# Home numbers for every expert in the dispatched rows, and one column of them fetched for each expert tile

## The chip, the cores and the metric

The kernel runs on one core of one Trainium2 chip. The metric is the device time of one execution in microseconds (us), the median of three runs. A core has TensorE (PE in the profile; PEld are its weight loads), VectorE (DVE), ScalarE (ACT), GpSimd (POOL) and SyncE (SP), and 16 DMA engines that serve the queues of all of them. SP only issues DMAs here, POOL issues the indirect ones.

## What is computed

Two transformer-like layers on one sequence of 2048 tokens of width 256, in float32. What matters here is the second:

```python
xn = _layernorm(x)
x = x + _L1_attn_ref(xn, W, b) + _L1_ffn_ref(xn, w_router, we1, we3, we2, ws1, ws3, ws2)

# _L1_ffn_ref: 16 experts, each token goes to its best 4
probs = softmax(xt @ w_router)
top_w, top_i = top_k(probs, 4)
top_w = top_w / sum(top_w)
g = silu(xt @ we1[e]) * (xt @ we3[e])          # 256 -> 128 for each expert e
moe_out = sum over the token's experts of top_w * (g @ we2[e])
shared = silu(xt @ ws1) * (xt @ ws3) @ ws2
out = shared / 5 + moe_out * 4 / 5
```

The attention of layer 1 is linear (one vector of sums over all tokens). Layer 0 has softmax attention with 16 heads and its own mixture of 16 experts with the best 2.

## The kernel before

Three stages follow each other, each a block of programs, one for each engine; the end of a block holds all engines until the last has finished.

**stage_first** (to about 602 us) is layer 0. Its work is interleaved by a planner written in Python. Only one step of it is touched: at a certain point SP clears rows of the scratch tensor xd1 in HBM (`clear`, L366 and L922).

**stage_second** (603 to 731 us) projects the attention output of layer 0, normalizes the 16 token tiles of 128 rows (four chunks of TC = 4 tiles), and routes. For each chunk VectorE picks the best four experts (`best_of`, which signals masks_ready), TensorE counts ranks (`ranks`, ranks_ready), and VectorE turns them into slots (`slots_of`, slots_ready): for each token and choice k the row of xd1 to which it goes. xd1 holds a region of CAP = 2048 + 128 rows for each expert. POOL then dispatches: for each chunk, choice and token tile one indirect DMA scatters 128 rows of `xn` (256 values, a one, and one more number) to xd1, 64 scatters in all. The additional number is the *home*: the row of yd1 where the result of this token and choice is to be written, token * 4 + k plus an offset. As it depends on k, POOL rewrites this column of xn for two tiles before each pair of scatters, and must first wait until the pair's earlier scatters have landed (L1848). SP meanwhile loads weights, copies padding rows behind the end of each expert's region (L1826), waits for the tables of the expert tiles (tables_ready) and for the whole dispatch (L1833), and loads the first four expert tiles into the ring `xs` (L1835). TensorE's main work from 651 on is the shared feed-forward part, 16 units (`shared`); VectorE multiplies each (`gated`).

**stage_experts** (731 us to the end) runs over NT1 = 79 tiles of 128 dispatched rows, each of one expert. For tile j TensorE transposes the rows of `xs` (L1694), ScalarE copies them out, TensorE makes the hidden part (L1702, eight products) with the weights that VectorE and ScalarE copied to `w_now` (L1569), ScalarE and VectorE make silu and product, TensorE the output (L1711), VectorE copies it to `ys` (L1651), and POOL scatters it to yd1 by the home numbers (L1682). The home numbers of a tile are made by POOL (L1676): the home column of xs, or a row of the ring's own dump area where the row is padding (it reads zero there). SP loads tile j into the ring of YRING = 4 as soon as tile j - 4 is transposed and its home numbers are made (L1582, L1583). The loop is unrolled by BODY = 16; at its head SP loads the first rows of the next 16 tiles into registers (L1576). After the loop the results are fetched in token order, weighted, summed and stored (L1588 to L1666), while TensorE makes the rest of the shared part.

## Time and profile before

| | |
|---|---|
| median of three runs | 906.23 us (905.91 to 911.66) |
| profiled execution | 906.89 us, its span 905.2 us |
| busy in the span: PE, DVE, ACT, POOL | 830.5, 645.3, 468.8, 437.1 us |
| stage_first, stage_second, stage_experts begin (first work on TensorE of the last two) | 0, 603.0, 731.3 us |
| mean granted TensorE clock | 0.96 of full speed |
| DMA packets, bytes | 70182, 110.05 MB |

Times in the rows are microseconds from the start of the span. The time between profiled time and span (1.7 us) lies outside the first and last instruction. The granted clock is 1.00 at 2.4 GHz and 0.50 at 1.2 GHz. A bracket at the end of a timeline row says how long the engine was idle before it and what ended the idle time; "issue" means that the profile shows nothing for which it waited.

### The profile page before, as it was taken

How to read it: one execution, taken by the hardware profiler on the slowest of the kernel's cores; microseconds unless marked ns; L12 is line 12 of the kernel's file. 1: busy time of each engine (PE TensorE's matmuls, PEld its weight loads, DVE VectorE, ACT ScalarE, POOL GpSimd, SP SyncE). 2: the span in 40 equal slices, each digit the busy share in tenths (PEclk: the TensorE clock that was granted, in tenths of full speed). 3: DMA queues.
4: the chain of work that ended last, by engine and by line, in shares of the span. 5: the costliest groups of instructions: out<-in, count | busy, mean ns of one | idle time of the engine just before them, and what ended most of it. 6: DMA issues, size and time to landing. Idle time of an engine off the chain costs nothing. (4 is left out here: it accounts for less than half of the span.)

```text
span 905.2 us, 16683 instructions
## 1 busy us (share of the span) xinstructions
PE 830.5 (92%) x4934; PEld 449.4 (50%) x4935; DVE 645.3 (71%) x1472; ACT 468.8 (52%) x883; POOL 437.1 (48%) x720
## 2 busy tenths in 40 slices
PE   5978699999988999999999998989999989999993
PEld 3533133334533444444444432138644769888982
DVE  5587988898867888888788888437547336555648
ACT  2643154556654666666565666754313046555547
POOL 3422045603652433653435446531578848878820
PEclk9997698999998999999999999989999989999997
DMA  9654772210272121272211222325852235555566
GB/s 328 212 129 137 207 142 89 89 46 25 81 128 71 49 61 56 80 127 71 70 38 38 55 60 76 93 65 188 302 166 88 88 117 164 157 154 159 158 255 246
DMA packets 70182, 110.05 MB, mean 122 GB/s; under 512 B 16662, under 2 KB 49942, under 8 KB 69590
## 3 DMA queue, kind: packets, MB, share of 16 engines
q1 hardware_dynamic: 49430, 54.04, 22.9%
q0 software_dynamic: 16000, 45.70, 14.7%
q10 hardware_dynamic: 4672, 9.34, 3.4%
q8 instruction: 38, 0.62, 0.3%
q14 instruction: 42, 0.34, 0.1%
HBM read 62.53 MB, written 46.22 MB: 120 GB/s over the span
## 5 line engine op out<-in xcount | busy, mean ns | idle before, releaser
L1275 DVE TENSOR_REDUCE part_max<-ps_row 128x1 f32<-128x512 f32 (+3 forms) x560 | 353.6, 670 | 71.1 <-PE ps_row L1429 38.7
L1139 ACT ACTIVATE probs<-ps_st 128x1024 f32<-128x1024 f32 (+3 forms) x320 | 278.2, 896 | 204.6 <-PE ps_st L1408 188.2
L1333 PE MATMUL ps_o<-probs,v_all 128*17 128x512 f32 (+3 forms) x1280 | 150.4, 542 | 6.9 <-POOL probs L1009 5.6
L1429 PE MATMUL ps_row<-ks,qs 96*128 96x512 bf16 (+3 forms) x320 | 110.2, 379 | 13.7 <-DVE part_max L1275 9.3
L1429 PE MATMUL ps_row<-xt_ks,qs 96*128 96x512 bf16 (+3 forms) x320 | 104.5, 354 | 6.9 <-DVE part_max L1275 6.5
L1682 POOL DMA_INDIRECT yd<-moe_ys,moe_home x79 | 82.6, 1046 | 25.5 <-POOL moe_home L1676 13.4
L1408 PE MATMUL ps_st<-qs,ks 99*128 99x512 bf16 (+3 forms) x320 | 88.7, 360 | 2.9 <-DMA qs<-max_parts 2.7
L1408 PE MATMUL ps_st<-qs,xt_ks 99*128 99x512 bf16 (+3 forms) x320 | 85.7, 356 | 3.9 <-ACT probs L1139 2.8
L1702 PE MATMUL moe_ps_h<-moe_xs_t,moe_w_now 128*128 128x128 f32 x632 | 86.0, 280 | 1.3 <-ACT moe_xs_t L1607 0.8
L1702 PEld LDWEIGHTS moe_ps_h<-moe_xs_t,moe_w_now 128*128 128x128 f32 x632 | 78.4, 195 | 3.2 <-DVE moe_w_now L1569 2.0
L1429 PEld LDWEIGHTS ps_row<-ks,qs 96*128 96x128 bf16 x320 | 31.9, 100 | 95.6 <-DVE part_max L1275 52.8
L1009 POOL TENSOR_SCALAR_AFFINE_SELECT probs<-probs 128x256 f32<-128x256 f32 x128 | 52.8, 419 | 47.3 <-ACT probs L1139 46.0
L1851 POOL DMA_INDIRECT xd<-xn,slot x64 | 65.8, 1029 | 19.0 <-issue 15.9
L1019 POOL TENSOR_SCALAR moe_h_tanh<-moe_h_tanh 128x128 f32<-128x128 f32 x47 | 25.0, 532 | 98.7 <-ACT moe_h_copy L1151 98.5
L1429 PEld LDWEIGHTS ps_row<-xt_ks,qs 96*128 96x128 bf16 x320 | 31.0, 97 | 80.7 <-DVE part_max L1275 46.6
L1642 DVE TENSOR_TENSOR moe_hid_t<-moe_ps_h,moe_act 128x128 f32<-128x128 f32 x79 | 23.0, 291 | 47.7 <-ACT moe_act L1614 37.2
L997 POOL DMA_INDIRECT xd<-o_t,slot x32 | 31.4, 982 | 46.2 <-ACT probs L1139 41.7
L1432 PE MATMUL ps_row<-mask,ident 128*128 128x128 bf16 x256 | 51.7, 227 | 0.0
L1711 PE MATMUL moe_ps_y<-we,moe_hid_t 128*128 x158 | 48.6, 389 | 3.1 <-DVE moe_hid_t L1642 1.6
L1408 PEld LDWEIGHTS ps_st<-qs,xt_ks 99*128 99x128 bf16 x320 | 27.3, 99 | 47.8 <-ACT probs L1139 27.0
L1029 POOL DMA_DIRECT2D yd<-moe_ys x47 | 28.5, 605 | 46.1 <-DVE moe_ys L1267 45.4
L1333 PEld LDWEIGHTS ps_o<-probs,v_all 128*17 128x17 f32 x1280 | 21.7, 95 | 53.6 <-issue 29.0
(288 smaller groups left out, 1307.3 us busy)
## 6 DMA issues: line engine op xcount, KB each, us to landing
moe_xs<-xd SPq DMA_DIRECT2D x79, 129.0 KB
qk_parts<-probs SPq DMA_DIRECT2D x16, 384.0 KB, 4.2
qs<-qk_parts SPq DMA_DIRECT2D x96, 64.0 KB, 2.5
moe_xs<-xd POOLq DMA_DIRECT2D x47, 128.0 KB, 2.4
yd<-moe_ys POOLq DMA_DIRECT2D x47, 128.0 KB, 2.1
xd<-zeros POOLq DMA_DIRECT2D x2, 2048.0 KB, 15.5
moe_w<-in_w ACTq DMA_DIRECT2D x2, 2048.0 KB
w<-in_we SPq DMA_DIRECT2D x8, 512.0 KB
```

Of the source, the lines that this page charges most:

```text
L997: pool.indirect_dma_start(out=m.xd0, out_offset=bass.IndirectOffsetOnAxis(m.r["slot"][:, choice, i:i + 1], 0), in_=m.xn[:, i, :], in_offse ...
L1009: pool.affine_select(out=corner, in_=corner, compare_op=ALU.is_ge, fill=keep, base=0, pattern=[[0, 2], [1, P]], channel_multiplier=-1).the ...
L1139: act.activation(probs[:, at % NPB, :, off:CH], ps_st[at % 2][:, :, off:CH], ACT.Exp, scale=HD ** -0.5).then_inc(exp_done, 1)
L1275: dve.tensor_reduce(part_max[reduced % 2][:, h:h + k, i, j:j + 1], bank[:, 0:k * w].rearrange("p (h w) -> p h w", h=k), AX_X, ALU.max).the ...
L1333: mm = pe.matmul(ps_o[32 * q:32 * q + HD + 1, off:CH], m.v_all[:, k, g * HG + q, :], probs[:, (at + q // 2) % NPB, q % 2, off:CH], start=F ...
L1408: mm = pe.matmul(ps_st[n % 2][:, h, off:CH], ks[g % 2][:, q, k * P:(k + 1) * P], qs[c][:, q, off:CH], start=True, stop=True)
L1429: mm = pe.matmul(cols, qs[c][0:KROWS, h, i * P:(i + 1) * P], ks[g % 2][0:KROWS, h, j * CH:j * CH + w], start=True, stop=(j < c))
L1432: mm = pe.matmul(cols[:, w - P:w], m.ident16[:, :], m.mask16[:, :], start=False, stop=True)
L1682: pool.indirect_dma_start(out=yd, out_offset=bass.IndirectOffsetOnAxis(home[:, k:k + 1].bitcast(U32), 0), in_=ys[:, k % U, :], in_offset=N ...
L1702: mm = pe.matmul(ps_h[b][:, part * P:(part + 1) * P], w_now[:, b, k, part * HID:(part + 1) * HID], xs_t[:, b, k, :], start=(k == 0), stop= ...
L1711: pe.matmul(ps_y[b][:, :], hid_t[:, b, :], w2[:, bass.ds(expert, 1), :], start=True, stop=True).then_inc(y_done, 1)
L1851: pool.indirect_dma_start(out=m.xd1, in_=xn[:, i, :], in_offset=None, out_offset=bass.IndirectOffsetOnAxis(r["slot"][:, k, i:i + 1], 0)).t ...
```

## The change

A row of xd1 now carries 16 home numbers, one for each expert (XW = D + 1 + E, 273 values instead of 258). For each chunk VectorE writes, for each token and expert e, token * 4 + (the choice k by which the token goes to e), from the masks of the choices, in three operations on 128 x 64 values (`homes_of`, at the start of `slots_of`). The numbers no longer depend on the choice that is being sent, so POOL writes no column and waits for no earlier dispatch: it issues the 64 scatters one after the other. In stage_experts SP loads the 256 values of each row and, by a second DMA of 128 pieces of 4 bytes, the one column that belongs to the tile's expert into `home` (`load_tile`). For this it loads the tile's expert into a register too. POOL's home numbers and the ring of dump rows go; the scatter of tile j takes the fetched column as its offsets and waits for the tile's loads (32 instead of 16). Padding rows and unused tiles get home numbers of their own in a larger dump area of yd1 (2 E tiles): SP writes them from `blank`, one DMA for the unused tiles, and the padding copies take the last block. The cleared part of xd1 grows from 1 block of 128 rows to 17.

```diff
-XW = D + 2
+XW = D + 1 + E
+PADS = E * (CAP + P)
...
-                        clear(sp, m, m.xd1, E * CAP // P, E * CAP // P + 1, m.cleared[1])
+                        clear(sp, m, m.xd1, E * CAP // P, PADS // P + 1, m.cleared[1])
...
+def load_tile(sp, m, b, j, first, expert):
+
+    sp.dma_start(m.xs[:, b, :], m.xd1[bass.ds(first, P), 0:D]).then_inc(m.x_in[b], 16)
+    sp.dma_start(m.home[:, j:j + 1] if isinstance(j, int) else m.home[:, bass.ds(j, 1)],
+                 m.xd1[bass.ds(first, P), bass.ds(expert + (D + 1), 1)].bitcast(I32),
+                 allow_slow_non_contiguous=True).then_inc(m.x_in[b], 16)
...
             def load_rows(j):
+                first_experts[:] = nc.values_load_multi_w_load_instructions(
+                    m.r["tile_e"][0:1, bass.ds(j + EPAD, BODY)], engines=[mybir.EngineType.SP], min_val=0,
+                    max_val=E - 1, skip_runtime_bounds_check_because=IN_RANGE)[1]
...
                 if there(j) and since(j, U):
                     sp.wait_ge(x_turned, j - (U - 1))
-                    sp.wait_ge(home_ready, j - (U - 1))
-                    sp.dma_start(xs[:, u % U, :], xd[bass.ds(first_rows[u], P), :]).then_inc(x_in[u % U], 16)
+                    load_tile(sp, m, u % U, j, first_rows[u], first_experts[u])
...
-            for j in range(tiles + 3):
-                if j < tiles:
-                    pool.wait_ge(x_in[j % U], 16 * (j // U + 1))
-                    pool.tensor_scalar(home[:, j:j + 1], xs[:, j % U, D + 1:XW], ring[:, j % U:j % U + 1], None,
-                                       ALU.max).then_inc(home_ready, 1)
-                k = j - 3
-                if k >= 0:
-                    pool.wait_ge(home_ready, k + 1)
-                    pool.wait_ge(y_copied, k + 1)
-                    pool.indirect_dma_start(out=yd, out_offset=bass.IndirectOffsetOnAxis(home[:, k:k + 1].bitcast(U32), 0),
-                                            in_=ys[:, k % U, :], in_offset=None).then_inc(y_out[k % U], 16)
+            for j in range(tiles):
+                pool.wait_ge(x_in[j % U], 32 * (j // U + 1))
+                pool.wait_ge(y_copied, j + 1)
+                pool.indirect_dma_start(out=yd, out_offset=bass.IndirectOffsetOnAxis(m.home[:, j:j + 1].bitcast(U32), 0),
+                                        in_=ys[:, j % U, :], in_offset=None).then_inc(y_out[j % U], 16)
...
-            sp.wait_ge(m.cleared[1], 16)
+            sp.wait_ge(m.cleared[1], 32)
+            sp.wait_ge(ones_ready, 3)
+            sp.dma_start(m.xd1[E * CAP:PADS + P, DP:XW].rearrange("(b p) h -> p b h", p=P), blank[:, :, :]).then_inc(m.cleared[1], 16)
+            sp.wait_ge(m.cleared[1], 48)
...
             for half in range(2):
                 sp.wait_ge(dispatched[half], 16 * TOP1 * T // 2)
+            experts = nc.values_load_multi_w_load_instructions(
+                m.r["tile_e"][0:1, EPAD:EPAD + YRING], engines=[mybir.EngineType.SP], min_val=0, max_val=E - 1,
+                skip_runtime_bounds_check_because=IN_RANGE)[1]
             for b, first in enumerate(rows):
-                sp.dma_start(m.xs[:, b, :], m.xd1[bass.ds(first, P), :]).then_inc(m.x_in[b], 16)
+                load_tile(sp, m, b, b, first, experts[b])
...
-                    for half in range(2):
-                        i = c * TC + 2 * half
-                        if k:
-                            pool.wait_ge(dispatched[half], 32 * (c * TOP1 + k))
-                        step.then(pool.tensor_copy(xn[:, i:i + 2, DP:XW], home[:, k, i:i + 2].unsqueeze(2)))
-                        for i in (i, i + 1):
-                            pool.indirect_dma_start(out=m.xd1, in_=xn[:, i, :], in_offset=None,
-                                                    out_offset=bass.IndirectOffsetOnAxis(r["slot"][:, k, i:i + 1], 0)
-                                                    ).then_inc(dispatched[half], 16)
+                    for i in range(c * TC, (c + 1) * TC):
+                        pool.indirect_dma_start(out=m.xd1, in_=xn[:, i, :], in_offset=None,
+                                                out_offset=bass.IndirectOffsetOnAxis(r["slot"][:, k, i:i + 1], 0)
+                                                ).then_inc(dispatched[i % 2], 16)
...
+            def homes_of(c):
+
+                k_hot, cs = r["hots"][c], slice(c * TC, (c + 1) * TC)
+                if c == 0:
+                    dve.wait_ge(homes_based, 1)
+                dve.wait_ge(masks_ready, c + 1)
+                step.then(dve.scalar_tensor_tensor(homes[:, :, :], k_hot[:, 2, :, :], 2.0, k_hot[:, 1, :, :], ALU.mult, ALU.add))
+                step.then(dve.scalar_tensor_tensor(homes[:, :, :], k_hot[:, 3, :, :], 3.0, homes[:, :, :], ALU.mult, ALU.add))
+                step.then(dve.tensor_tensor(xn[:, cs, DP:XW].bitcast(I32), homes[:, :, :],
+                                            home[:, cs].unsqueeze(2).to_broadcast([P, TC, E]), ALU.add))
+
             def slots_of(c):
 
+                homes_of(c)
                 chunk_slots(dve, step, r, c, ranks_ready, slots_ready)
```

## Rows read from the trace of the kernel before

**Rows 1.** Timeline of all engines at the hand-over to stage_experts: start, duration, engine, line.
```profile
725.96 0.97 POOL L1851 DMA_INDIRECT xd<-xn,slot  x1 [0.30 <-issue]
727.29 0.69 DVE L1992 TENSOR_TENSOR o_t<-ps_ab,gate 128x512 f32<-128x512 f32 x1 [2.74 <-issue]
728.66 1.95 SPq L1835 DMA_DIRECT2D moe_xs<-xd  x4
...
731.28 1.09 PE L1694 MATMUL moe_ps_x<-ident,moe_xs 128*128 128x128 f32 x4 [4.10 <-PEq L1734]
```

**Rows 2.** Windows of 1 us: busy time of each engine, granted clock, DMA share, GB/s.
```profile
core 0: us, PE busy (x) PEld busy (x) DVE busy (x) ACT busy (x) POOL busy (x), PEclk, DMA share, GB/s
...
604.00:605.00 1.00, 1.00 (x3) 0.75 (x3) 0.42 (x1) 0.00 (x0) 0.00 (x0) 0.50 0.28 62
...
729.00:730.00 1.00, 0.00 (x0) 0.00 (x0) 0.00 (x0) 0.00 (x0) 0.00 (x0) 0.98 0.26 61
...
736.00:737.00 1.00, 1.00 (x6) 0.97 (x5) 0.00 (x0) 0.25 (x1) 0.00 (x0) 0.61 0.54 140
```

**Rows 3.** POOL's two operations of an expert tile: duration ns min/median/max, first and last start.
```profile
L1682 POOL DMA_INDIRECT yd<-moe_ys,moe_home x79: 974/1047/1107, 738.5 to 866.2; - x79
L1676 POOL TENSOR_SCALAR moe_home<-moe_xs,moe_ring x79: 280/300/417, 731.6 to 861.3; 128x1 int32<-128x1 f32 x79
```

**Rows 4.** TensorE's timeline, the transposes of two expert tiles, four tiles apart.
```profile
750.99 0.38 PE L1694 MATMUL moe_ps_x<-ident,moe_xs 128*128 128x128 f32 x2
...
757.18 0.38 PE L1694 MATMUL moe_ps_x<-ident,moe_xs 128*128 128x128 f32 x2
```

**Rows 5.** Waits from 731 to 865: who for whom, us in total, times, longest.
```profile
PE moe_ps_h L1702 <- DVE moe_w_now L1569: 0.4, 1, 0.4
...
PEld moe_ps_h L1702 <- DVE moe_w_now L1569: 2.0, 4, 0.7
```

**Rows 6.** POOL's dispatch: the page's row (busy, mean ns, idle before), then its timeline.
```profile
L1851 POOL DMA_INDIRECT xd<-xn,slot x64 | 65.8, 1029 | 19.0 <-issue 15.9
...
625.89 1.01 POOL L1851 DMA_INDIRECT xd<-xn,slot  x1 [0.58 <-POOL xn L1849]
...
634.38 0.19 POOL L1849 CAST xn<-home 128x2 f32<-128x2 int32 x1 [3.46 <-DMA xd<-xn,slot]
```

**Rows 7.** Timeline of all engines at the hand-over from stage_first to stage_second.
```profile
601.88 0.59 ACT L1050 COPY masks<-ps_o 128x512 f32<-128x512 f32 x1 [1.18 <-PE ps_o L1333]
...
602.99 0.67 PE L2129 MATMUL ps_o<-count,o_t 128*128 128x256 f32 x2 [1.16 <-PEq L776]
```

**Rows 8.** POOL's timeline, the last scatter of the results.
```profile
866.18 0.97 POOL L1682 DMA_INDIRECT yd<-moe_ys,moe_home  x1 [0.30 <-issue]
```

**Rows 9.** VectorE's timeline in stage_second.
```profile
640.60 0.22 DVE L268 COPY given<-ps_l 128x64 f32<-128x64 f32 x1 [1.63 <-PE ps_l L246]
...
663.09 0.23 DVE L295 SCALAR_TENSOR_TENSOR weight<-weight,top_sum 128x64 f32<-128x64 f32 x1
```

**Rows 10.** TensorE's timeline, the transposes of tiles 12 and 13 in stage_second.
```profile
638.26 0.60 PE L2098 MATMUL ps_t<-ident,xn 128*128 128x128 f32 x4
```

**Rows 11.** SP in the loop over expert tiles: its waits, and its register loads.
```profile
SPq L1583 <- POOL moe_home L1676: 64.3, 65, 2.4
...
L1576 SPq TENSOR_LOAD <-tile_row x5: 284/977/990, 731.1 to 833.3; - x5
```

**Rows 12.** DMA issues: engine, count, KB each, median us from issue to landing.
```profile
moe_xs<-xd POOLq DMA_DIRECT2D x47, 128.0 KB, 2.4
...
xd<-zeros POOLq DMA_DIRECT2D x2, 2048.0 KB, 15.5
...
w_router<-in_w_router SPq DMA_DIRECT2D x1, 16.0 KB, 1.7
```

**Rows 13.** SP's timeline in stage_first around the clearing of xd1.
```profile
191.35 0.59 SPq L371 DMA_DIRECT2D xd<-zeros  x1
209.08 1.77 SPq L865 DMA_DIRECT2D qs<-max_parts  x3
```

**Rows 14.** VectorE's copies of the weights in the loop: ns min/median/max.
```profile
L1569 DVE COPY moe_w_now<-w x79: 293/351/569, 731.8 to 861.0; 128x256 f32 x79
```

41 lines of the change are left out of this document (20 added, 21 removed).

## The prediction

> **What bounds the kernel now.** I read the profile in the order in which the change touches it. First the page's 40 slices and the windows: TensorE is busy nearly without a break through both late stages, so a microsecond counts only if it moves TensorE or the hand-over from one stage to the next. Then the timeline of all engines at the hand-over from stage_second to stage_experts [rows 1]. VectorE's last product starts at 727.29 and ends at 727.98. POOL's last dispatch starts at 725.96, so its rows land after 727. SP waits for them, starts its first row load at 728.66 and is through with four of them at 730.61. Only then does every engine pass the end of the block: TensorE's first transpose is at 731.28, after 4.10 us of nothing. TensorE had ended at 727.18, VectorE at 727.98, so about 3 us of the pause belong to the dispatch and the loads behind it. The windows show a second price [rows 2]: the granted clock still reads 0.98 in 729 to 730, is 0.50 afterwards, and comes back within 736 to 737. The first expert tiles run at 1.2 GHz.
>
> In stage_experts the chain of waits names POOL from 807 on, scatter and home number in turn. That is a trap. POOL needs 1.05 us for a scatter and 0.30 for a home number [rows 3], and with the gaps about 1.56 per tile; TensorE passes four tiles in 757.18 - 750.99 = 6.19 us, 1.55 per tile [rows 4]. The two run side by side, but the waits of TensorE and its weight loads in this stretch name neither a transfer nor POOL; beside the hand-over the largest is 2.0 us in total for VectorE's weight copies [rows 5]. TensorE sets the pace and POOL only follows.
>
> **What the change removes.** (1) In the dispatch POOL now writes a home column (0.19 us) before each pair of scatters, and from the second choice on waits until the last scatters of these rows have landed; one such wait was 3.46 us [rows 6]. Without column and waits, 64 scatters take 1.03 us each in the mean and some 0.3 between them [rows 6], 85 us. From 625.89, and 0.75 later for the new VectorE work below, they end near 712. The last rows land before 716, and SP's eight short issues are done by about 720. That is 8 us ahead of VectorE's 727.98. The dispatch thus leaves the path, and the hand-over waits for VectorE. How long the block's end then takes is seen at the stage before: ScalarE ended at 602.47, TensorE began at 602.99, 0.52 us [rows 7]. So TensorE begins at 727.98 + 0.52 = 728.5 instead of 731.28: **-2.8 us**.
>
> (2) The pause shrinks from 4.1 to 1.3 us, and with it, I hold, the low clock disappears. The mean of 0.98 in 729 to 730 [rows 2] says that the clock was full until close to 730, 2.8 us into the pause. Against it: after the pause of 1.16 us at 602.99 [rows 7] the granted clock is 0.50 in 604 to 605 [rows 2]; but there TensorE came out of a stretch with gaps and narrow products, here out of one that the slices show as full. From 731.28 to the fourth tile's transpose near 737.1 pass 5.8 us. TensorE does in it two tiles' work less one output product, plus one pair of transposes: at the pace of 1.55 us [rows 4] about 2.9 us, and 0.6 that I allow for ScalarE's first copies, 3.5 in all. Bounds 0 and 2.5; I take **-2.3 us**, as the full clock at 729 to 730 is the nearer row.
>
> (3) In stage_experts 79 home numbers of 0.30 us [rows 3] leave POOL, and SP's wait for them. POOL drops to about 1.35 per tile, but TensorE's 1.55 stays: worth 0. The end also stays: the last scatter at 866.18 stood only behind its predecessor's issue, 0.30 us [rows 8], and no home number was there.
>
> **What it adds.** (4) VectorE makes the columns: three small operations on 128x64 per chunk. The nearest row is the scalar_tensor_tensor on 128x64, 0.23 us, 0.25 with its wait [rows 9]: 0.75 us per chunk. homes_of stands ahead of the wait for the ranks. In chunks 2 and 3 VectorE waits there for TensorE, 1.63 us in chunk 2 [rows 9] and more in chunk 3: hidden. In chunk 0 later gaps of VectorE take it up. In chunk 1 nothing does: the deviations of chunk 3 and best_of(2) stand behind it, the transposes of tiles 12 and 13 start at 638.26 [rows 10], just as their rows come, and the ranks of chunk 2 right after best_of(2). From there on TensorE has no slack up to 727: **+0.75 us**, bounds 0 (if the gaps take it) and 1.5 (two chunks exposed).
>
> (5) SP issues two DMAs per tile. An issue with its register work takes 1.95 / 4 = 0.48 us [rows 1], so 0.96 per tile against 1.55: SP keeps up, with 0.59 in hand. SP waits 64.3 us in total for home numbers now, about 1 us per load [rows 11]; once they are gone it goes on the transposes alone. A load is wanted four tiles later: 6.19 us, less 0.38 for the transposes [rows 4], 0.48 for the row's issue ahead of the column's and 0.2 that I allow for hops, leaves 5.1 us for the column to land. Every 16 tiles SP loads 16 experts besides 16 rows. One load is 0.98 us [rows 11]; two, and 0.6 that I allow for the jump, less the 0.59 in hand, make the next column 2.0 us late: 3.1 us are left there. A DMA of 256 short pieces landed in 1.7 us, a 128 KB row load in 2.4 [rows 12]: hidden, by 0.7 us at the worst place. Cost 0; bounds 0 and 4 us (four loop heads, 1 us each, if the column takes 4.1).
>
> (6) The clearing of xd1 on SP grows from 0.13 to 2.4 MB, at 191.35, and SP's next transfer is at 209.08 [rows 13]. 2 MB took 15.5 us at the kernel's start beside other loads [rows 12]; 17.7 are free: hidden, bounds 0 and 1. The block of blank home numbers, the padding copies and wider rows (1092 for 1032 bytes) stand on SP and the DMA engines between 634 and 701, when SP waits for the tables: hidden. POOL's three new small operations before 625 meet an idle engine.
>
> **Sum.** -2.8 - 2.3 + 0.75 = -4.35. Against the profiled execution's 906.89 us (span 905.2) that is 902.5; it lies 0.66 above the median of 906.23, against which the change gives **901.9 us**.
>
> **Two rules weighed.** The loop's copies of the weights on VectorE take 293 ns at best and 569 at worst [rows 14], while POOL always works beside them. The Trainium skill, "SBUF — State Buffer", Who interferes with whom, says that a VectorE copy in a two-port mode and a GpSimd instruction lock each other out for a whole instruction. By it the missing home numbers would free VectorE; by the row the median is 351 ns, near the best, so most copies are nearly free already. The time is rival C's.
> The 256 pieces that landed in 1.7 us [rows 12] speak for a cheap column. The Trainium skill, "DMA: Bandwidth & Descriptors", Specifications and Rules for kernel authors, speaks against this change: a strided last dimension becomes one descriptor per element, and below 512 bytes a write becomes read-modify-write. By it 128 pieces of 4 bytes could land later than the row itself; the time of that is rival D's.
>
> **Rivals.**
> A. The clock falls all the same: the pause of 1.16 us at 602.99 is the row for it. Only terms 1 and 4 remain: 906.23 - 2.8 + 0.75 = 904.2.
> B. The gain is given back in stage_experts, as the column is late at the loop heads (4 us, term 5), or the columns cost VectorE two exposed chunks, or the dispatch takes so much longer inside its scatters that it still ends last. The first gives 905.9, the last 906 to 907. Against the last: 8 us of room.
> C. Fewer lockouts between POOL and VectorE: TensorE's weight loads no longer wait for the copies. 79 x (351 - 293 ns) is 4.6 us of VectorE, but TensorE stands behind few of them: 2.0 + 0.4 us [rows 5] are the most, 899.5.
> D. Slower: the column becomes the bound of the ring of four. From 5.1 us of landing on it decides; each us more costs 1/4 us per tile. At 6.0 us: 75 x 0.22 = 17 us, 919. For 1% slower it needs 5.8 us. Rows of 1.7 and 2.4 us [rows 12] speak against it.
>
> **Chances.** Forecast (terms 1 to 4 as priced, 900.5 to 903) 0.43; A 0.23; B 0.15; C 0.11; D 0.08. One per cent, 9 us, is about what a measurement of this kernel tells from no change. Faster by over 1% would need twice the sum: 0.04. Slower is D with little else: 0.08. Same: 0.88. The range holds forecast, A, C and most of B, with 1 us either way for the unlike loop stalls: 899.0 to 908.0. D is left out.
>
> **What would show it.** Right: no wait for landed dispatches in POOL's dispatch, which ends before 716; SP's first row load before 722; TensorE's pause at the hand-over 1.2 to 1.5 us, first transpose near 729.3 (728.5 + 0.75); granted clock 1.00 throughout 730 to 737; the transposes of tile 12 about 0.7 later; 1.55 us per tile in the loop, POOL with 0.2 us of idle per tile. Wrong: a clock of 0.50 after the hand-over (A); TensorE waiting for xs at tiles 16, 32, 48 or 64 (B) or everywhere (D); weight copies near 293 ns with a shorter loop (C); SP's loads still issued after 727; TensorE waits in attention between 191 and 209.

## The result: 7.5% slower, and the profile after

The changed kernel took 972.91 us (median; 970.61 to 981.85) against 908.94 for the kernel before on the same chip, a ratio of 1.0747 (95%: 1.0703 to 1.0791). The ratios leave out executions more than 1.5% above the fastest of the same kernel, such as one of 937.38 us among the four of the kernel before, which is in the median of 908.94 (the other three took 905.91 to 911.66); the profile of e12 below is of such an execution and isn't used. The profiled execution of the changed kernel took 972.37 us, its span is 970.6 us, 65.4 more than the span before. By stages, read from TensorE's first work in each and the last transpose of an expert tile:

| us | before | after | difference |
|---|---|---|---|
| until stage_second | 603.0 | 600.7 | -2.3 |
| stage_second | 128.3 | 174.6 | +46.3 |
| stage_experts to the last transpose | 128.7 | 150.6 | +21.9 |
| the rest | 45.2 | 44.7 | -0.5 |

The page after, busy tenths of the span in 40 slices, TensorE, then GpSimd, then the granted clock:

```profile
PE   5887889899979999999999988963589998888894
POOL 3322066425524336434354464267530044444520
PEclk9997689999989999999999999968699999999998
```

The same line of TensorE in the page before:

```profile
PE   5978699999988999999999998989999989999993
```

TensorE has a hole in slices 27 to 29 (631 to 704 us), where before it was busy without a break, and there GpSimd is busy. The windows of 5 us show it closer (busy time of PE, PEld, DVE, ACT, POOL; clock; DMA share; GB/s):

```profile
660.00:665.00 5.00, 2.37 (x14) 1.28 (x14) 2.58 (x18) 0.00 (x0) 3.89 (x4) 1.00 0.31 112
...
675.00:680.00 5.00, 0.00 (x0) 0.00 (x0) 0.00 (x0) 0.00 (x0) 3.78 (x5) 0.50 0.31 112
680.00:685.00 5.00, 0.00 (x0) 0.00 (x0) 0.00 (x0) 0.00 (x0) 3.78 (x5) 0.50 0.31 112
...
690.00:695.00 5.00, 4.83 (x6) 2.18 (x7) 2.43 (x8) 3.54 (x5) 0.31 (x1) 0.50 0.00 0
```

TensorE, VectorE and ScalarE all stand still while GpSimd issues scatters, and the DMA engines are busy to 31% only. What do they wait for? The longest waits from 628 to 730:

```profile
DVE given L269 <- remote: 38.1, 2, 28.9
ACT gram L1888 <- remote: 37.3, 1, 37.3
...
PE ps_gram L2207 <- ACT gram L1888: 23.5, 1, 23.5
```

"remote" means that an increment of a semaphore ended the wait, but that no instruction ended near it. Both waits are for TensorE. The timelines of TensorE, ScalarE, VectorE and GpSimd:

```profile
656.40 3.71 PE L2134 MATMUL ps_gram<-xn 128*128 128x257 f32 x16
...
664.80 1.88 PE L2199 MATMUL ps_t<-xt,ws 128*128 128x512 f32 x4
...
685.54 0.97 POOL L1855 DMA_INDIRECT xd<-xn,slot  x1 [0.31 <-issue]
686.82 0.97 POOL L1855 DMA_INDIRECT xd<-xn,slot  x1 [0.30 <-issue]
...
689.47 0.65 ACT L1888 COPY gram<-ps_gram 128x257 f32<-128x257 f32 x2 [37.28 <-remote]
...
690.17 6.25 PE L2207 MATMUL ps_gram<-w_attn,gram 128*128 128x512 f32 x8 [23.49 <-ACT gram L1888]
...
692.40 0.23 DVE L269 COPY given<-ps_ab 128x64 f32<-128x64 f32 x1 [28.92 <-remote]
...
694.69 0.97 POOL L1855 DMA_INDIRECT xd<-xn,slot  x1 [6.90 <-DVE slot L281]
```

The gram products end at 660.12, ScalarE copies them at 689.47. The semaphore records of the trace give the reason: TensorE's increments arrive late. For some of the products that increment a semaphore, the end as the profile models it and the time of the increment:

```
product (line)            ends               its increment arrives
ranks, chunk 1 (L247)     629.12             644.73
logits, chunk 2 (L2122)   629.55 to 636.33   644.79, 644.85, 644.91, 644.97
gram (L2134)              660.12             689.45
ranks, chunk 3 (L247)     663.16             692.31
shared, first (L2193)     664.96             692.37
shared, second (L2199)    666.68             692.43
```

Products that ended microseconds apart report 0.06 us after one another, in order, and the two bunches come 2.5 and 4.5 us after the last scatter of a chunk has ended on GpSimd (642.25 and 687.79). I read it so: the products had long been computed, and their increments stood in a queue. That is a reading, as the trace models the ends of products and does not measure them. Nor is the queue shut altogether while GpSimd issues: between 655.74 and 660.71 four increments of the logits of chunk 3 arrive, 0.5 to 4.2 us late. Increments of VectorE and ScalarE in the same stretch are within 0.03 us of their instructions. While TensorE stands, its clock falls to 0.50, which costs again when it goes on.

The loop of stage_experts shows the same on a smaller scale. Its groups (busy, mean ns, idle before and what ended it):

```profile
L1681 POOL DMA_INDIRECT yd<-moe_ys,moe_home x77 | 74.8, 972 | 140.6 <-DVE moe_ys L1659 114.2 <-issue 26.5
L1710 PE MATMUL moe_ps_y<-we,moe_hid_t 128*128 x158 | 50.3, 400 | 19.5 <-DVE moe_hid_t L1650 19.1 <-issue 0.3
L1575 DVE COPY moe_w_now<-w 128x256 f32 x79 | 23.7, 300 | 9.7 <-issue 5.8 <-PEq L1733 1.1
```

And its waits (us in total, times, longest):

```profile
DVE moe_hid_t L1650 <- ACT moe_act L1622: 49.8, 36, 3.6
ACT moe_act L1622 <- PE moe_ps_h L1701: 39.5, 35, 2.4
```

The same products in the loop before:

```profile
L1711 PE MATMUL moe_ps_y<-we,moe_hid_t 128*128 x158 | 48.6, 389 | 3.1 <-DVE moe_hid_t L1642 1.6 <-issue 1.4
```

TensorE waits 19.1 us for the hidden part (1.6 before). ScalarE waits 39.5 for `moe_ps_h` (29.5 before), whose increment is the late one. GpSimd sends three scatters 1.3 us apart, then finds no rows, because the increments that would bring them are held; it pauses, they come, and it begins again:

```profile
907.35 0.97 POOL L1681 DMA_INDIRECT yd<-moe_ys,moe_home  x1 [2.44 <-DVE moe_ys L1659]
908.62 0.97 POOL L1681 DMA_INDIRECT yd<-moe_ys,moe_home  x1 [0.30 <-issue]
909.94 0.97 POOL L1681 DMA_INDIRECT yd<-moe_ys,moe_home  x1 [0.34 <-issue]
...
913.32 0.97 POOL L1681 DMA_INDIRECT yd<-moe_ys,moe_home  x1 [2.41 <-DVE moe_ys L1659]
```

So the theory: **TensorE's semaphore increments are held up while GpSimd issues indirect DMAs too densely; the removed waits and small operations had kept the scatters apart.** The rivals: the transfers themselves (more in flight, wider rows, the blank pieces), the column fetch in the loop, and later that it is the chip. The expectations below number the theories: 1, an operation between scatters lets the increments through; 2, the transfers hold them back; 3, the column fetch slows the loop; 4, the mean interval between scatters decides, with an excess that builds up; 5, it is two scatters with nothing between them; 6, only waits for landed scatters help; 7, it is also the chip.

### The profile page after: what moved, and what is told of

Its sections match the earlier page's. It is cut to its first block and busy times, and to the rows that moved or that the text cites. A ratio compares the mean times of both kernels' runs of the same rounds, so it can differ in the third digit from the quotient of the medians.

```text
span 970.6 us, 16726 instructions
## 1 busy us (share of the span) xinstructions
PE 843.0 (87%) x4934; PEld 454.5 (47%) x4935; DVE 641.7 (66%) x1484; ACT 468.3 (48%) x883; POOL 396.8 (41%) x610
## 5 line engine op out<-in xcount | busy, mean ns | idle before, releaser
L1681 POOL DMA_INDIRECT yd<-moe_ys,moe_home x79 | 76.8, 972 | 141.2 <-DVE moe_ys L1659 114.2
L1855 POOL DMA_INDIRECT xd<-xn,slot x64 | 62.2, 973 | 51.1 <-DVE slot L281 32.5
L1430 PEld LDWEIGHTS ps_row<-ks,qs 96*128 96x128 bf16 x320 | 32.2, 101 | 95.0 <-DVE part_max L1276 52.4
L1710 PE MATMUL moe_ps_y<-we,moe_hid_t 128*128 x158 | 50.3, 400 | 19.5 <-DVE moe_hid_t L1650 19.1
L1622 ACT ACTIVATE moe_act<-moe_ps_h 128x128 f32<-128x128 f32 x79 | 22.0, 279 | 56.2 <-PE moe_ps_h L1701 42.1
```

Source lines behind the costliest of these rows:

```text
L1430: mm = pe.matmul(cols, qs[c][0:KROWS, h, i * P:(i + 1) * P], ks[g % 2][0:KROWS, h, j * CH:j * CH + w], start=True, stop=(j < c))
L1681: pool.indirect_dma_start(out=yd, out_offset=bass.IndirectOffsetOnAxis(m.home[:, j:j + 1].bitcast(U32), 0), in_=ys[:, j % U, :], in_offset ...
L1710: pe.matmul(ps_y[b][:, :], hid_t[:, b, :], w2[:, bass.ds(expert, 1), :], start=True, stop=True).then_inc(y_done, 1)
L1855: pool.indirect_dma_start(out=m.xd1, in_=xn[:, i, :], in_offset=None, out_offset=bass.IndirectOffsetOnAxis(r["slot"][:, k, i:i + 1], 0)).t ...
```

## The experiments

"Late" below counts increments of TensorE more than 0.4 us behind the modelled end of the last product before them that reports to the same semaphore; where several are held back at once this makes the delay too small, never too large. The column has the number in stage_second and in the loop, then the longest of each in us. "Interval" is the mean distance in us of the last 16 scatters of the dispatch. Runs e1 to e4 shared a chip, as did e5 to e8, e9 to e12, e13 to e16, e17 and e18. Ratios are to the kernel before on the same chip.

| run | edit | interval | stage_second, loop (us) | late in each, longest | ratio (95%) |
|---|---|---|---|---|---|
| before | | 1.49 | 128.3, 128.7 | 2, 44; 1.1, 1.6 | |
| changed | | 1.28 | 174.6, 150.6 | 20, 73; 29.3, 2.9 | 1.0747 |
| e1 | operation per pair; in loop one each | 1.35 | 174.4, 126.9 | 21, 39; 22.9, 1.5 | 1.0505 (1.0445 to 1.0566) |
| e2 | landing waits; no column fetch | 1.28 | 172.1, 144.3 | 7, 67; 43.6, 2.7 | 1.0587 (1.0500 to 1.0673) |
| e3 | before, no waits | 1.28 | 176.2, 128.6 | 22, 41; 17.6, 1.6 | 1.0502 (1.0381 to 1.0624) |
| e4 | no blank pieces | 1.28 | 174.6, 148.6 | 19, 74; 31.1, 2.9 | 1.0743 (1.0610 to 1.0876) |
| e5 | operation per pair and landing waits | 1.40 | 129.8, 122.9 | none | 1.0037 (1.0018 to 1.0057) |
| e6 | operation before each | 1.62 | 126.7, 126.2 | none | 1.0064 (1.0038 to 1.0089) |
| e7 | two per pair; no column fetch | 1.63 | 127.6, 126.3 | none | 1.0050 (1.0030 to 1.0070) |
| e8 | before, waits, no operation | 1.34 | 123.9, 121.5 | none | 0.9925 (0.9896 to 0.9954) |
| e9 | changed | 1.27 | 172.8, 148.2 | 20, 77; 32.2, 2.3 | 1.0738 (1.0700 to 1.0776) |
| e10 | as e6 | 1.64 | 130.0, 126.3 | 21, 49; 3.8, 1.4 | 1.0055 (0.9994 to 1.0116) |
| e11 | as e3 | 1.27 | 170.0, 127.8 | 22, 36; 29.1, 1.4 | 1.0479 (1.0390 to 1.0568) |
| e12 | landing waits; operation in loop | not used | not used | not used | 1.0456 (1.0367 to 1.0546) |
| e13 | as e6, in loop ahead of the wait | 1.62 | 127.8, 126.3 | none | 1.0054 (1.0033 to 1.0076) |
| e14 | two per pair | 1.63 | 128.3, 127.2 | none | 1.0073 (1.0049 to 1.0096) |
| e15 | changed | 1.43 | 124.2, 121.4 | none | 0.9945 (0.9922 to 0.9969) |
| e16 | as e5, in loop one each | 1.40 | 132.1, 126.1 | none | 1.0097 (1.0061 to 1.0134) |
| e17 | before | 1.45 | 125.6, 133.1 | 4, 53; 1.8, 2.2 | 0.9942 (0.9861 to 1.0022) |
| e18 | as e14 | 1.63 | 128.2, 130.8 | 4, 44; 0.8, 1.7 | 0.9964 (0.9901 to 1.0027) |

### e1 to e4: GpSimd's pace against the transfers

**e1.** In the dispatch and in the loop:

```diff
                     for i in range(c * TC, (c + 1) * TC):
+                        if i % 2 == 0:
+                            step.then(pool.tensor_copy(gap[:, 0:2], home_i[:, 0:2]))
                         pool.indirect_dma_start(...)
...
                 pool.wait_ge(y_copied, j + 1)
+                pool.tensor_scalar(gap[:, 1:2], gap[:, 0:1], 0.0, None, ALU.max).then_inc(gap_sem, 1)
+                pool.wait_ge(gap_sem, j + 2)
                 pool.indirect_dma_start(...)
```

> The changed kernel with one idle GpSimd operation put back at the two places where the change removed one: in the dispatch a copy of 128x2 into a scratch tile before each pair of scatters (no wait for landed scatters), in stage_experts an operation on 128x1 into a scratch tile before each scatter. Everything else, home columns, blank home numbers and the column fetch, stays. Nothing of the computation is left out. Theory 1 (TensorE's semaphore increments do not get through while GpSimd issues indirect DMAs with nothing between them; an operation between lets them through): stage_second falls from 174.6 to about 128 us, stage_experts up to the last transpose from 150.6 to about 129, together 904 to 910 us, and no increment of TensorE comes more than 2 us after its matmul. Theory 2 (the transfers themselves, scatters without landing waits and the blank pieces, hold the increments back): stage_second stays near 174, since as many transfers are in flight as before. Theory 3 (the loop is slow because of the column fetch): the loop stays near 150. By 2 and 3 the time stays at 968 to 976.

Measured 948.85 us. The loop is healed, 150.6 to 126.9, by an operation whose result nobody reads; TensorE's wait for the hidden part in it is 0.3 us. The dispatch is not: 174.4.

```profile
L1686 POOL DMA_INDIRECT yd<-moe_ys,moe_home x77 | 79.4, 1031 | 25.9 <-POOL moe_gap L1684 14.4 <-issue 7.7 <-DVE moe_ys L1660 3.7
L1715 PE MATMUL moe_ps_y<-we,moe_hid_t 128*128 x157 | 48.3, 389 | 1.1 <-issue 0.5 <-DVE moe_hid_t L1651 0.3
```

**e2.** The old waits alone, and a loop without column fetch:

```diff
+                        if k and i % 2 == 0:
+                            pool.wait_ge(dispatched[i // 2 % 2], 32 * (c * TOP1 + k))
...
-    sp.dma_start(m.home[:, j:j + 1] ..., m.xd1[..., expert + (D + 1)] ...).then_inc(m.x_in[b], 16)
```

> The changed kernel with two edits in different stages. In the dispatch the old waits for the earlier scatters of the same two tiles are put back, without a GpSimd operation. In stage_experts the column fetch is left out, and the scatters take home numbers that are made once before the dispatch (tile * 128 + partition), so the rows of the results are not those of the tokens; the scatters follow each other as in the changed kernel. Theory 1: the dispatch is healed if a wait between scatters is enough to let TensorE's increments through (stage_second about 128), and is not if only an operation does (about 174); the loop stays slow (about 150 to the last transpose), as GpSimd still has nothing between its scatters: 925 or 970 us in all. Theory 2: stage_second about 128, as fewer transfers are in flight. Theory 3: the loop falls to about 129 us, with the dispatch healed 905 us in all.

962.48 us. The waits hold GpSimd back only while the weights are loaded. From 656 on nothing waits any more:

```profile
645.32 0.97 POOL L1855 DMA_INDIRECT xd<-xn,slot  x1 [4.62 <-DMA xd<-xn,slot]
...
656.26 0.97 POOL L1855 DMA_INDIRECT xd<-xn,slot  x1 [0.99 <-DMA xd<-xn,slot]
657.54 0.97 POOL L1855 DMA_INDIRECT xd<-xn,slot  x1 [0.30 <-issue]
```

TensorE is busy nearly throughout up to 665, and stands from 690 to 715. Its products that end at 664.72, 666.43, 668.15 and 676.32 report at 704.48, 715.68, 719.90 and 719.96: matched one by one, the third is 51.8 us late (the table's way of counting gives 43.6 as the longest). Three increments of this stretch arrive while GpSimd still issues (671.97, 682.67, 704.48), the others from 3.2 us after its last scatter on. So the stall does not need the crowded stretch; it comes with the interval of 1.28 us. Theory 3 falls too: without the column the loop still takes 144.3.

**e3.** The kernel before, its dispatch set free:

```diff
-                        if k:
-                            pool.wait_ge(dispatched[half], 32 * (c * TOP1 + k))
-                        step.then(pool.tensor_copy(xn[:, i:i + 2, DP:XW], home[:, k, i:i + 2].unsqueeze(2)))
```

> The kernel before with its dispatch set free: the home column of a chunk is written once instead of before each pair of scatters, and the waits for landed scatters are gone, so GpSimd issues 16 scatters of a chunk one after the other. Rows stay 258 wide, there are no blank home numbers and no column fetch. The home numbers in the rows are therefore those of the first choice only; stage_experts makes its home numbers, by the same GpSimd operation as before, from a fixed table instead of from the rows, so the results land in other rows. Theory 1: TensorE's increments are held back as in the changed kernel, stage_second grows from 128 to about 170 us, the loop stays as before: 945 to 955 us. Theory 2 in the form that the wider rows or the blank pieces do it: stage_second stays at 128 or shrinks by the 5 us of the prediction, 900 to 908 us in all. Theory 2 in the form that the number of scatters in flight does it: as theory 1.

949.25 us, stage_second 176.2, the loop 128.6 as before. The home column is written once for each chunk, and the loop takes its home numbers from a fixed table, so the results land in other rows. Rows of 258, no homes on VectorE, no blank pieces, no column: on this chip, taking away GpSimd's pauses is enough for the whole loss of stage_second.

**e4.**

```diff
-            sp.dma_start(m.xd1[E * CAP:PADS + P, DP:XW].rearrange(...), blank[:, :, :]).then_inc(m.cleared[1], 16)
-            sp.wait_ge(m.cleared[1], 48)
```

> The changed kernel without the DMA of the blank home numbers (2176 pieces of 64 bytes, issued from 630.13 to 642.14 by SP). The columns are fetched as before, but the scatters of stage_experts take fixed home numbers (tile * 128 + partition), so the results land in other rows. Theory 1: only the share of SP and of the first stretch changes; stage_second stays 165 to 175 us, the loop near 150, 962 to 972 us in all. Theory 2 in the form that the blank pieces block the DMA engines: stage_second falls to about 128 us, 925 us in all.

The scatters of the loop take fixed home numbers here, so the results land in other rows. 968.25 us, stage_second 174.6: the blank pieces are no part of it. Against e2, the column fetch costs the stalled loop 4.3 us, where two profiles of the changed kernel's loop differ by 2.4 (150.6, and 148.2 in e9).

### e5 to e8: slower paces

e5 has e1's operation and e2's wait before each pair, e6 the operation before every scatter, e7 twice before each pair:

```diff
-                        if i % 2 == 0:
-                            step.then(pool.tensor_copy(gap[:, 0:2], home_i[:, 0:2]))
+                        step.then(pool.tensor_copy(gap[:, 0:2], home_i[:, 0:2]))
```

e8 is the kernel before with its operation for k = 0 only:

```diff
                         if k:
                             pool.wait_ge(dispatched[half], 32 * (c * TOP1 + k))
-                        step.then(pool.tensor_copy(xn[:, i:i + 2, DP:XW], home[:, k, i:i + 2].unsqueeze(2)))
+                        else:
+                            step.then(pool.tensor_copy(xn[:, i:i + 2, DP:XW], home[:, k, i:i + 2].unsqueeze(2)))
```

> The changed kernel with GpSimd's dispatch paced exactly as before: in front of each pair of scatters one copy of 128x2 (into a scratch tile) and, from the second choice on, the wait for the landed scatters of these two tiles. In stage_experts an operation on 128x1 stands before every second scatter only. Nothing of the computation is left out. Theory 4 (GpSimd issues scatters faster than something in the chip takes them; TensorE's increments wait behind the excess, so the mean interval decides, and the landing waits take the excess away in the stretch in which the weights are loaded): stage_second 126 to 132 us, as before, and no increment over 2 us late in it; the loop, at a mean interval of 1.4 us where GpSimd has rows waiting, lies between the two seen (127 and 150). If stage_second stays near 174, it is the wider rows or something else of the change, not GpSimd's pace. In all 904 to 925 against 948.

> The changed kernel with an idle GpSimd operation before every single scatter, in the dispatch (copy of 128x2) and in stage_experts (128x1), and no landing waits. Nothing of the computation is left out. Mean interval in the dispatch about 1.45 us against 1.36 with one operation for each pair and 1.28 in the changed kernel. Theory 4 (mean interval): the increments get through except in the stretch from 620 to 650, in which the weights are loaded and the excess builds up; stage_second 135 to 160. Theory 5 (two scatters with nothing between them hold the increments back): healed altogether, stage_second 126 to 130, 900 to 905 us in all. Theory 6 (only landing waits help): about 174, 948 us in all.

> The changed kernel with two idle GpSimd operations before each pair of scatters in the dispatch (mean interval about 1.5 us, but the two scatters of a pair still follow each other with nothing between), no landing waits. In stage_experts an operation before each scatter, and no column fetch: the scatters take fixed home numbers, so the results land in other rows. Theory 4: stage_second as with an operation before each scatter (135 to 160 us, or healed). Theory 5: about 174 us, as with one operation for each pair. The loop shows the price of the column fetch where GpSimd's pace is not the trouble: 126.9 us with it; the same without if it is hidden, 122 to 125 if it costs what the comparison of 144.3 with 148.6 and 150.6 us suggests.

> The kernel before with the landing waits of its dispatch kept, but the copy of the home column done for the first choice of a chunk only; after that each pair of scatters has only the wait before it. The home numbers in the rows are those of the first choice, and stage_experts makes its home numbers by the same operation from a fixed table, so the results land in other rows. Rows stay 258 wide, no blank numbers, no column fetch. Theory 4: GpSimd falls into an interval of 1.28 us once the weights are loaded, and stage_second grows to about 172 us, as in the changed kernel with landing waits; 945 to 955 us in all. If it stays at 128, the wider rows are part of the cause.

898.68, 901.50, 900.89 and 890.08 us, with 895.63 for the kernel before. No late increment in any, not even in e8, for which theory 4 had said 945 to 955 (interval 1.34 us at the end, 1.28 in the median). That is a miss, and none of the four could be read without knowing whether this chip holds increments back at all. What can be read: the column fetch costs nothing in a loop without stalls (126.2 with it, 126.3 without), and one idle operation for each tile costs 3 to 5 us of loop here (e5 with half as many 122.9; e8, which makes home numbers on GpSimd three tiles ahead, 121.5). They also move the end of the dispatch back: the last scatter starts at 719.6 in e6, against 714.1 in e8, and TensorE's pause at the hand-over is 3.55 us against 1.35.

### e9 to e16: the same kernels beside the changed one

e9 and e15 are the changed kernel, e10 is e6, e11 is e3. e12 has e2's waits and e1's loop, e13 is e6 with the loop's operation moved, and SP loads the first tiles' experts into registers before it waits for the dispatch instead of after:

```diff
+                gaps.then(pool.tensor_scalar(gap[:, 1:2], gap[:, 0:1], 0.0, None, ALU.max))
                 pool.wait_ge(x_in[j % U], 32 * (j // U + 1))
                 pool.wait_ge(y_copied, j + 1)
```

e14 and e16 have this loop and this order on SP too, with the dispatches of e7 and e5.

> The changed kernel itself, unedited, on the chip of the three runs beside it. The four runs before this one showed no late increment of TensorE at all, in stages in which the earlier runs had many, so either their edits healed it (an operation between the scatters, or landing waits) or that chip does not show it. By theory 4 (GpSimd's pace against what the chip takes) the changed kernel runs at 960 to 975 us here as well, stage_second about 174 us, increments up to 30 us late. By theory 7 (the increments are late only on some chips or at some times, whatever GpSimd does) it runs at 900 to 915 us where the kernel before shows none late.

> The kernel with an idle GpSimd operation before every scatter in both stages, again, now on the same chip as the changed kernel. Theory 4: stage_second 127 to 130 us and no late increment, wherever it runs, about 900 us. Theory 7: as the changed kernel on this chip, less what the operation does: if that one has increments up to 30 us late, this has too (stage_second over 160).

> The kernel before without the landing waits and with one home column for each chunk (258 wide rows, home numbers of the first choice only, results at fixed rows), again, on the same chip. Theory 4: stage_second about 174 us, 945 to 955 us. Theory 7: where the chip shows no late increment, the hand-over comes early and stage_second takes 124 us, 888 to 892 us in all.

> The changed kernel with the old landing waits in the dispatch (no operation between the scatters) and an idle GpSimd operation before each scatter of stage_experts. Nothing of the computation is left out. Theory 4: the dispatch runs at 1.28 us a scatter from 656 on and stage_second takes 172 us as in the second run, the loop 127: about 944 us. Theory 7: on a chip without late increments the dispatch ends near 712, stage_second takes 124 to 126 us and the loop 123 to 127: 893 to 899 us.

969.79, 909.39, 944.24 and 947.88 us, with 905.87 before. On this chip the changed kernel stalls, and one idle operation before each scatter takes 60 us off it: stage_second 172.8 to 130.0, the loop 148.2 to 126.3, the longest delay 32.2 to 3.8. e9 and e10 are the cleanest pair, as they ran beside each other and differ in the idle operations alone. The wait of ScalarE for the gram products, e9 first, then e10:

```profile
ACT gram L1888 <- remote: 39.4, 1, 39.4
...
ACT gram L1896 <- PE ps_gram L2142: 7.5, 1, 7.5
```

Not all of e10's expectation came: it has 21 late increments in stage_second where none was expected. Theory 6 falls with e10, which has no landing waits. Landing waits alone (e12, by its time) don't heal the dispatch.

> Meant as the best version: the changed kernel with an idle GpSimd operation before each scatter of the dispatch, and in stage_experts the idle operation before each scatter too, but ahead of the wait for the copied output, where it costs the chain nothing; SP loads the expert registers before it waits for the dispatch. Nothing of the computation is left out. Theory 4: stage_second 126 to 130 us, loop 123 to 126: equal to the kernel before on this chip within 1%, 3 us below the version with the operation behind the wait.

> As the version with an idle operation before each scatter, but in the dispatch two idle operations stand before each pair of scatters and none between the two of a pair: the same mean interval of about 1.45 to 1.5 us. Nothing of the computation is left out. If the changed kernel stalls on this chip: theory 4 (mean interval) says stage_second 126 to 132 us; theory 5 (two scatters with nothing between them) says about 170 us, as with one operation for each pair. If the changed kernel does not stall here, this run tells nothing of the two.

> The changed kernel itself, unedited, beside the others on this chip. Theory 4 alone: 965 to 975 us, stage_second 172 to 175 us. Theory 7 (it is also the chip): either that, or, on a chip like that of the runs without a late increment, stage_second 124 to 127 us and 893 to 900 us in all.

> The changed kernel with the dispatch paced exactly as before (an idle operation and the landing wait before each pair of scatters) and in stage_experts an idle operation before each scatter, ahead of the wait for the copied output. Nothing of the computation is left out. Theory 4: no increment over 2 us late in stage_second, 127 to 131 us; loop 123 to 126; equal to the kernel before within 1%. If the wider rows, and not GpSimd's pace, were behind the loss, stage_second would be over 160 us wherever the changed kernel is slow.

901.13, 901.74, **890.75** and 904.78 us, with 895.49 before. Here the unedited changed kernel is faster than the kernel before, by 0.55% (0.31 to 0.78), without one late increment, and every idle operation only costs. So e13, e14 and e16 can't test theories 4 and 5 or the wider rows here. It is not the pace that spares this chip: e15's scatters come 1.27 us apart in the median, as in the stalled runs (its mean of the last 16 is 1.43, as VectorE works and some of them take longer). The same kernel is held up on one chip and not on the other, as theory 7 says. But no chip was measured twice, so what belongs to the chip and what to the time at which it was measured isn't told apart. The changed kernel's hand-over on this chip, first the timeline, then windows of 2 us:

```profile
704.62 0.97 POOL L1855 DMA_INDIRECT xd<-xn,slot  x1 [0.30 <-issue]
...
707.75 0.38 SPq L1507 DMA_DIRECT2D moe_xs<-xd  x1
708.39 0.37 SPq L1508 DMA_DIRECT2D moe_home<-xd  x1
...
722.75 0.69 DVE L2008 TENSOR_TENSOR o_t<-ps_ab,gate 128x512 f32<-128x512 f32 x1 [2.74 <-PE ps_ab L2199]
...
723.99 0.63 PE L1693 MATMUL moe_ps_x<-ident,moe_xs 128*128 128x128 f32 x4 [1.34 <-PEq L1733]
...
727.75 0.38 PE L1693 MATMUL moe_ps_x<-ident,moe_xs 128*128 128x128 f32 x2
```

```profile
724.00:726.00 2.00, 1.37 (x11) 1.17 (x12) 0.59 (x2) 1.26 (x4) 0.00 (x0) 1.00 0.00 0
726.00:728.00 2.00, 2.00 (x19) 1.90 (x18) 0.76 (x3) 1.30 (x5) 0.00 (x0) 1.00 0.30 71
```

### e17 and e18

e17 is the kernel before, e18 is e14.

> The kernel before, unedited, profiled. Theory 7 on a chip that delays increments: as in its first trace, stage_second 128 to 130 us, stage_experts 128 to 129 us to the last transpose, about 40 increments of TensorE 0.4 to 1.6 us late in the loop, 901 to 910 us (or a second level near 928). On a chip that does not: no late increment, the loop 121 to 122 us, stage_second about 128 us with TensorE's pause of 4.1 us at the hand-over, 893 to 898 us.

> Two idle GpSimd operations before each pair of scatters of the dispatch, none between the two of a pair; in stage_experts one before each scatter. Nothing of the computation is left out. On a chip whose kernel before shows late increments in the loop: theory 4 (mean interval 1.5 us) says stage_second 127 to 133 us and about 908 us in all; theory 5 (adjacent scatters hold the increments back) says about 170 us and about 948. On a chip that shows none it runs at 900 to 902 us and tells nothing of the two.

The kernel before shows 53 late increments in its loop (up to 2.2 us, 133.1 us) on this chip, so it holds increments back there; the changed kernel was not run on it, so that it would have stalled in the dispatch is assumed. e18 has 128.2 us of stage_second and 909.06 us in all. Its scatters, two of them adjacent:

```profile
705.32 0.19 POOL L1861 CAST e_gap<-home_i 128x2 f32<-128x2 int32 x1
705.58 0.18 POOL L1862 CAST e_gap<-home_i 128x2 f32<-128x2 int32 x1
706.04 0.96 POOL L1863 DMA_INDIRECT xd<-xn,slot  x1 [0.28 <-issue]
707.31 0.96 POOL L1863 DMA_INDIRECT xd<-xn,slot  x1 [0.30 <-issue]
```

So adjacent scatters were harmless here, and theory 5 falls, as far as that assumption holds. On the chips that hold increments back, dispatches at 1.27 to 1.35 us stalled (seven profiles), those at 1.45 to 1.64 did not (four). The chip's part in it was not found.

This is not a threshold. The kernel before owes its 1.49 to two intervals of 2.08 and 2.64 us; from 708.32 on its last 14 scatters go in e1's very pattern:

```profile
713.77 0.97 POOL L1851 DMA_INDIRECT xd<-xn,slot  x1 [0.28 <-issue]
715.05 0.97 POOL L1851 DMA_INDIRECT xd<-xn,slot  x1 [0.31 <-issue]
716.02 0.20 POOL L1849 CAST xn<-home 128x2 f32<-128x2 int32 x1
716.50 0.97 POOL L1851 DMA_INDIRECT xd<-xn,slot  x1 [0.28 <-issue]
```

That is 1.36 us in the mean for 18 us (e1: 1.35), and the four increments recorded in it (709.97 to 725.48) are within 0.02 us. In e1 increments are 4.7 us late within 12 us of the first scatter, in the stretch in which the weights are loaded and in which the kernel before waits for landings (4.90 and 3.79 us between scatters). So the interval alone doesn't decide; what came before it does too, as theory 4 has it, or the wider rows, which differ as well between these two: the changed kernel with e5's dispatch (e5, e16) was never run on a chip that holds increments back. The interval may moreover be in part an effect: while VectorE stands, GpSimd's small operations take 0.20 us (e1), where before some took 0.38 and 0.46.

No version was shown to beat the kernel before on both kinds of chip: the changed kernel wins 0.55% on one and loses 7.4 to 7.5% on the other; e10's and e18's are level with it there, and e13's and e14's cost 0.5 and 0.7% on the first.

## Why the prediction was wrong

**Terms 1 and 3, the place of the error.** The step that failed is in term 1, "Without column and waits, 64 scatters take 1.03 us each [...] The dispatch thus leaves the path", and again in term 3, "POOL drops to about 1.35 per tile, but TensorE's 1.55 stays: worth 0". I asked who waits for GpSimd, and never what GpSimd's own pace does to the others. GpSimd's forecast was right to a few us (last scatter before 716 wanted, 713.8 measured, although its slots came late), and the 46.3 and 21.9 us came on engines of which the change had removed nothing. Shown in its place, by e9 and e10: GpSimd's denser issue, priced at nothing for TensorE, holds TensorE's increments back by up to 32 us, and spacing it takes the 60 us away. Why the increments queue stays open. A sign of it stood in the trace of before: its loop is 1.63 us per tile, while four tiles in a quiet place pass at 1.55 [rows 4]. I took the difference for unlike stalls. It goes with the late increments (44 in that loop): where there are none, a loop with the same operations takes 121.5 us (e8, 1.54 per tile) instead of 128.7. No rival held it; D is on the right side, with the wrong mechanism.

**Where increments are not held back, the sum holds.** e15 gives -0.55% (-0.78 to -0.31), the prediction -0.48%. That it agrees so well is in part luck: no kernel before was profiled on such a chip, so its pause at the hand-over is not known there (4.10 us in [rows 1], but 2.29 in e17), and the clock could as well have fallen. By its points:
- Term 1: the last scatter starts at 704.62, the loads at 707.75. TensorE starts 0.55 us after VectorE's last product (0.52 forecast), and its pause is 1.34 us (1.2 to 1.5 forecast; 4.10 in [rows 1]). Shown in e15; e8, the kernel before with an earlier dispatch, has the same pause (1.35) and gains 0.75% (0.46 to 1.04).
- Term 2: the clock is 1.00 in every window from 720 to 736, and from the first transposes to the fourth tile's pass 3.76 us; 3.5 were forecast, and 5.8 had passed before, where the clock fell to 0.50 [rows 2]. Against before that is 2.0 us, where term 2 has 2.3. But the full clock was luck. Ten profiles have a pause of 1.34 or 1.35 us here. In four of them the clock fell to 0.50 soon after it (the changed kernel's first, e2, e3, e9), in six it stayed at 1.00 (e1, e4, e8, e10, e11, e15); beside e1 to e4 as beside e9 to e11 both happened on one chip. Where it fell, the fourth tile comes after 5.36 to 5.41 us, and little of term 2 is left. So rival A, with a chance of 0.23, came true in four of ten, and no run shows what decides it.
- Term 3: the loop at 121.4 us, as in e8, whose loop is that of before (121.5). Worth 0, as said.
- Term 4: `homes_of` takes 0.85 us in e15 (634.75 to 635.60), 0.75 forecast:

```profile
634.75 0.22 DVE L1960 SCALAR_TENSOR_TENSOR homes<-masks 128x64 f32<-128x64 bf16 x1
635.01 0.22 DVE L1961 SCALAR_TENSOR_TENSOR homes<-masks,homes 128x64 f32<-128x64 bf16 x1
635.27 0.30 DVE L1962 TENSOR_TENSOR xn<-homes,home 128x64 int32<-128x64 f32 x1
```

- Term 5: cost 0 forecast with a bound of 4. e15's loop has three waits of TensorE's weight loads for the column:

```profile
PEld moe_ps_x L1693 <- DMA moe_home<-xd: 2.0, 3, 1.0
```

  The Trainium skill, "DMA: Bandwidth & Descriptors", Rules for kernel authors, speaks of one descriptor per element for a strided last dimension; the column of 128 pieces was never the bound of the ring (e6 against e7: 0.1 us), so rival D's condition did not come.
- Term 6: hidden, but I had not priced SP. The DMA of 2176 pieces of 64 bytes keeps SP for 11.74 us in e15 and 12.01 in the changed kernel's first profile, the 16 padding copies 24.11 instead of 12.86 in that profile, but 11.73 in e15. In e15 SP still waits 28.1 us for the tables after it.

**Rival C.** VectorE's weight copies fell from a mean of 374 to 300 ns (23.7 us in 79). The Trainium skill, "SBUF — State Buffer", Who interferes with whom, says that a VectorE copy in a two-port mode and a GpSimd instruction lock each other out. The traces agree, as far as such copies are in that mode: with an idle operation back before each scatter the mean is 333 to 339 ns (e1, e10, e13), without one 300 to 314. It was worth nothing: TensorE did not stand behind them.

## What to carry to other kernels

A wait or a small operation between DMAs of GpSimd can be a brake that others live on. Before removing it, ask not only who waits for GpSimd, but what its denser issue does to TensorE's semaphore increments, and look for waits marked "remote" and for products that ended long before their reader starts. If TensorE's readers start late while its rows are on time, try spacing the scatters (here an operation before each, 1.44 us from one to the next at least) before hunting for the transfer. And measure on more than one chip before a change of 0.5% is believed: this one was -0.55% on one and +7.4% on the next.

## What the runs showed of the hardware

- Increments of TensorE can arrive 43.6 us after their product and more (e2; 51.8 where matched one by one), in order, and then 0.06 us apart; those of VectorE and ScalarE beside them were within 0.03 us (first profile of the changed kernel). Delays of over 4 us in the dispatch were seen only with scatters of GpSimd at a mean interval of 1.35 us or less, while the DMA engines were busy to 31% only (675 to 685 us of the changed kernel); that interval alone was not enough (last 18 us of the dispatch before).
- It happened on the chips of four of the six measurements and on two not once, with the changed kernel and e6's edit tried on both kinds. Whether the chip or the time makes the difference is open. The scatters' own transfers don't show it: from 650 to 660 us the queue of GpSimd moves 384 packets in e9, which stalls, and 461 in e15, which doesn't, at 181 and 179 ns each in the median.
- After one and the same pause of TensorE, 1.34 to 1.35 us, the granted clock fell to 0.50 in four profiles and stayed at 1.00 in six.
- The stall may feed itself: with VectorE standing, GpSimd's operations take their shortest times (interval 1.35 in e1, where the same pattern took 1.49 in the whole of the last 16 scatters before), so the scatters come denser. No run tests this alone.
